# Causal convolution of a Mamba block moved from VectorE to ScalarE products and accumulating transfers

## The reference, cut to what matters

```python
x = x + 0.5 * ffn(layernorm(x))      # 8 experts, all dense: silu(x Wg) * (x Wu) Wd, weighted per row
x = x + mamba(layernorm(x))
x = x + 0.5 * ffn(layernorm(x))      # the same weights again
```

```python
xs, z = jnp.split(x @ W_in, 2, axis=-1)
xc = silu(depthwise_conv(xs, conv_w, 4 taps, causal) + conv_b)   # the change is here
dbl = xc @ W_x                                                   # 64 for dt, 16 for B, 16 for C
dt = softplus(dbl[:, :64] @ W_dt + b_dt)
h_t = exp(dt * A) * h_(t-1) + (dt * xc) * B_t                    # 16 states a channel
y = (sum over states of h_t * C_t + xc * D) * silu(z)
out = y @ W_out
```

## Time and profile before

| | before |
|---|---|
| three runs, us | 1270.12, 1273.47, 1273.81 (median 1273.47) |
| span of the profiled execution, us | 1272.6 |
| PE busy, us (share of the span) | 1253.2 (98%) |
| DVE busy | 1114.1 (88%) |
| ACT busy | 926.6 (73%) |
| POOL busy | 394.3 (31%) |
| chain that ended last, by engine | PE 73%, DVE 8%, DMA 8%, issue 5%, ACT 3%, POOL 2% |
| DMA: bytes moved, mean rate | 182.96 MB, 144 GB/s |
| queue of GpSimd's transfers, share of the 16 engines | 45.9% |
| mean granted TensorE clock | 0.998 |

### The profile page before, as it was taken

The page is one execution under the profiler, slowest core; times in us unless marked ns, Lnnn a source line. Parts: engine busy times, 40 slices in busy tenths (PEclk is TensorE's granted clock), DMA queues, the critical chain, the costliest instruction groups (busy, mean ns, idle before and its releaser), DMA issues.

```text
span 1272.6 us, 21027 instructions
## 1 busy us (share of the span) xinstructions
PE 1253.2 (98%) x7584; PEld 1096.0 (86%) x7584; DVE 1114.1 (88%) x1481; ACT 926.6 (73%) x1778; POOL 394.3 (31%) x459
## 2 busy tenths in 40 slices
PE   7999999999999999999999999999999999999998
PEld 5888888888888888888888888888888888888887
DVE  4544899989999999999999999999999989999433
ACT  5645978978886978877968788798867968654421
POOL 0101333334342423343333433333334333332110
PEclk9999999999999999999999999999999999999999
DMA  8211677777788868787987878887978887895111
GB/s 244 52 26 30 146 155 154 147 154 158 152 180 164 170 132 183 159 165 161 180 177 150 166 164 176 158 168 148 186 157 167 163 165 142 163 183 107 35 33 33
DMA packets 109303, 182.96 MB, mean 144 GB/s; under 512 B 11024, under 2 KB 23824, under 8 KB 109200
## 3 DMA queue, kind: packets, MB, share of 16 engines
q0 software_dynamic: 56336, 102.79, 45.9%
q1 hardware_dynamic: 52864, 78.85, 24.7%
HBM read 76.22 MB, written 2.62 MB: 62 GB/s over the span
## 4 chain that ended last, share of the span: by engine, by line
PE 73%; DVE 8%; DMA 8%; issue 5%; ACT 3%; POOL 2%; SPq 0%; DVEq 0%; POOLq 0%; ACTq 0%
PE PS L700 27%; PE PS L643 14%; PE PS L646 14%; PE PS L644 14%; DMA Y<-HS 5%; DVE HB L825 2%; DVE HS L923 2%; DMA XS<-DX 2%; DVE HS L931 1%; PE PS L730 1%; PE PS L715 1%; DVE HS L912 1%; PE PS L658 1%; POOL Y L1137 1%; DVE YE L818 1%
## 5 line engine op out<-in xcount | busy, mean ns | idle before, releaser
L700 PEld LDWEIGHTS PS<-WD,HB 128*128 128x128 f32 x4096 | 536.6, 191 | 44.0 <-issue 1.5
L700 PE MATMUL PS<-WD,HB 128*128 128x128 f32 x4096 | 540.1, 275 | 0.0
L1016 ACT ACTIVATE HB<-PS 128x512 f32<-128x512 f32 x512 | 294.3, 596 | 272.9 <-PE PS L646 270.8
L825 DVE TENSOR_TENSOR HB<-PS,HB 128x512 f32<-128x512 f32 x512 | 348.7, 682 | 119.2 <-PE PS L646 110.9
L1137 POOL DMA_DIRECT2D Y<-HS x252 | 221.1, 972 | 383.7 <-DVE HS L931 262.7
L1120 POOL DMA_DIRECT2D XT<-YE x126 | 117.9, 936 | 433.2 <-DVE YE L818 407.4
L643 PE MATMUL PS<-XH,WG 128*128 128x512 f32 x512 | 244.5, 478 | 3.3 <-ACT XH L996 2.3
L643 PE MATMUL PS<-XH,WU 128*128 128x512 f32 x512 | 204.9, 400 | 0.0
L646 PE MATMUL PS<-XH,WG 128*128 128x512 f32 x512 | 203.2, 397 | 0.6 <-DVE XH L883 0.6
L646 PE MATMUL PS<-XH,WU 128*128 128x512 f32 x512 | 202.1, 395 | 0.0
L644 PE MATMUL PS<-XH,WG 128*128 128x512 f32 x512 | 201.0, 393 | 0.0
(11 more groups left out here) (109 smaller groups left out, 1080.9 us busy)
## 6 DMA issues: line engine op xcount, KB each, us to landing
BCB<-BCD SPq DMA_DIRECT2D x128, 512.0 KB, 5.3
Y<-HS POOLq DMA_DIRECT2D x252, 256.0 KB, 6.4
XT<-YE POOLq DMA_DIRECT2D x126, 256.0 KB, 4.4
XS<-DX POOLq DMA_DIRECT2D x7, 512.0 KB, 9.2
XT<-in_L_attn_x_dram SPq DMA_DIRECT2D x8, 256.0 KB, 6.5
WD<-in_L_ffn_w_down_dram SPq DMA_DIRECT2D x8, 256.0 KB, 4.8
out_dram<-XT SPq DMA_DIRECT2D x8, 256.0 KB, 5.6
HS<-in_L_ffn_w_gate_dram SPq DMA_DIRECT2D x6, 256.0 KB, 4.0
```

The lines of the kernel that those rows point to most:

```text
L700: z = pe.matmul(expert(g)[:, j, :], HB[:, i % NH, j * P:(j + 1) * P], WD[:, e, c, :], start=c == 0 and j == 0, stop=c == FC - 1 and j == S ...
L825: v.tensor_tensor(H, up(i), H, ALU.mult).then_inc(S["v_h"], 1)
L1016: a.activation(HB[:, i % NH, :], gate(i), ACT.Silu).then_inc(S["a_sil"], 1)
```

## The change

For tiles 1 to 7 the multiply-adds of `b_conv` on DVE are replaced. Tile 0 keeps them. For each tap q = 0, 1, 2 and half j, ACT writes a product XS[q : q + 512] * tap q into a new buffer TP[q, j] (`b_tap`). GpSimd adds them with accumulating transfers of 128 x 512 f32, which is 256 KB: TP[0, j] += TP[1, j], and Y[j] += TP[2, j], both issued in `b_tap`; then, once both have landed, Y[j] += TP[0, j] (`b_sum`). The semaphore `c_cv0` or `c_cv1` counts the three landings of its half; `b_silu` waits for all three, and `b_sum` for the first two. `b_dt` waits for ACT's own products (`a_cv`) before XS is overwritten. In the planner a product costs .72 on ACT and needs a `calm()`, a transfer .95 on GpSimd and 5.0 more until it has landed. There are now a `yield` after each product and each sum, and an `until(at)` for the landing before the sums.

```diff
@@ before(t)
         for q in range(3):
             for j in range(2):
+                if t:
+                    yield from calm()
+                    at = step("b_tap", t, q, j, after=win_at, a=.72)
+                    if q:
+                        clock["p"] = max(clock["p"], at) + .95
+                        at = clock["p"] + 5.0
+                    yield True
+                    continue
                 at = step("b_conv", t, q, j, v=.67)
                 if q != 1:
                     yield True
             if q < 2:
                 bk = yield from take()
                 give(bk[0], "a_win", 4 * t + q + 3, step("b_in", t, q + 2, bk, pe=.69, a=.52))
+                yield True
+        if t:
+            yield from until(at)
+            for j in range(2):
+                at = step("b_sum", t, j, p=.95) + 5.0
                 yield True
         yield from until(at - .5)
@@ macaron_program
+        TP = sb("TP", [P, 3, 2, T])
@@ ACT
+                elif k == "b_tap":
+                    _, t, q, j = s
+                    wt.wait_ge(S["a_win"], 4 * t + 2)
+                    wt.wait_ge(S["v_halo"], 2 * t + 1)
+                    if t > 1:
+                        wt.wait_ge(S[f"c_cv{j}"], 16 * 3 * (t - 1))
+                    a.activation(TP[:, q, j, :], XS[:, t % 2, j, q:q + T], ACT.Copy, scale=cw_t[:, j, q:q + 1]).then_inc(S["a_cv"], 1)
                 elif k == "b_silu":
                     _, t, j = s
                     y = Y[:, t % 2, j, :]
-                    wt.wait_ge(S["v_cv"], 6 * t + 4 + j + 1)
+                    if t:
+                        wt.wait_ge(S[f"c_cv{j}"], 16 * 3 * t)
+                    else:
+                        wt.wait_ge(S["v_cv"], 4 + j + 1)
                     a.activation(y, y, ACT.Silu, bias=cb_t[:, j:j + 1]).then_inc(S["a_yc"], 1)
@@ ACT, b_dt
-                    wt.wait_ge(S["v_cv"], 6 * t + 6)
+                    if t:
+                        wt.wait_ge(S["a_cv"], 6 * t)
+                    else:
+                        wt.wait_ge(S["v_cv"], 6)
@@ GpSimd
+                elif k == "b_tap":
+                    _, t, q, j = s
+                    if q:
+                        wt.wait_ge(S["a_tap"], 2 * t + j + 1)
+                        wt.wait_ge(S["a_cv"], 6 * (t - 1) + 2 * q + j + 1)
+                        to = TP[:, 0, j, :] if q == 1 else Y[:, t % 2, j, :]
+                        gp.dma_start(to, TP[:, q, j, :], accum_op=ALU.add).then_inc(S[f"c_cv{j}"], 16)
+                elif k == "b_sum":
+                    _, t, j = s
+                    wt.wait_ge(S[f"c_cv{j}"], 16 * (3 * t - 1))
+                    gp.dma_start(Y[:, t % 2, j, :], TP[:, 0, j, :], accum_op=ALU.add).then_inc(S[f"c_cv{j}"], 16)
```

More of the change, by code:

```diff
@@ L499, in macaron_program @@
         S = {}
-        for n in ("c_small c_con c_wr c_acc c_y0 c_y1 c_bcd c_dt o_x init w_hi w_lo dv "
+        for n in ("c_small c_con c_wr c_acc c_y0 c_y1 c_bcd c_dt c_cv0 c_cv1 a_cv o_x init w_hi w_lo dv "
                   "m_g m_u m_dn m_tr m_lg m_win m_wx m_wt m_wo "
```

## The result

The changed kernel takes 1320.31 us (median of four runs, 1319.5 to 1323.3) against 1273.17 us for the kernel before (1270.12 to 1273.81). The ratio is 1.038, 95% interval 1.037 to 1.040: 47 us slower. The direction was forecast, the size was not: 1287 us and a range up to 1305. The span of the profiled execution is 1317.9 us, 45.3 more than before.

What follows compares the result with a forecast made beforehand. PE's full queue was taken as the bound, with DVE's chain just below. From 1272.6 us: minus 1 for DVE's relief, plus 9 for W_x stalls, plus 6 for the last tile, 1286.6, stated as 1287; range 1273 to 1305.

Steps and rivals of the forecast that it cites:

- The bound: Over the whole kernel, PE's queue sets the end; other engines' gains can return at most 9.5 us.
- ACT's products at nothing: 42 products on ACT, 30.3 us in all, fit its free time through calm() and cost 0.
- The chain after the last product: In each convolution, from last product towards W_x: two landings and one issue, 13.7 us, bounds 7.5 and 22.7.
- The stalls at W_x: PE waits at W_x for landings longer than planned: 1.3 us in each of 7 tiles, 9 us, bounds 0 and 28.
- Tiles 2 to 6 "no harm": In tiles 2 to 6 a later convolution does no harm, since their scans were not waiting for DX.
- Rival 3: Transfers served late, GpSimd and ACT queues held up, PE losing 3 us or more per tile: about 1308 us; chance 0.16.
- The last tile: Tile 7 has no slack: its scans start 8 us later, costing 6 us at the end, bounds 0 to 12.
- the 6 us between W_x and DX: In tile 7, W_x to DX shrinks by 6 us from 29.3, as tile 6's scans end sooner; between 0 and 8.
- DVE's relief at 1 us: DVE loses 31.3 us of multiply-adds; with PE full, only 1 us of PE's 9.5 us of waits is credited.
- my own two terms, 28 and 12 us: Upper bounds of the PE stalls at W_x over seven tiles (28) and the last tile's wait at the end (12).

Runs made afterwards that it cites:

- e13: The changed kernel with the calm() before each product taken out and nothing else: 1305.2 us, ratio 1.028 to the kernel before.
- e12: The changed kernel's work relisted: products one after another, three calm() instead of six, W_in's z chunks during the landings, usual turns: 1295.8 us, ratio 1.019.
- e6: The list of the kernel before with the changed work: products on ACT, accumulating transfers, nothing planned for landings: 1354.8 us, ratio 1.065.
- e5: The changed kernel's list, but DVE keeps the multiply-adds, with no products and no added transfers: 1330.5 us, ratio 1.046.
- e2: The change for tiles 1 to 6 only; tile 7 keeps DVE's multiply-adds: 1323.7 us, ratio 1.041 to the kernel before.
- e1: The change for tile 7 alone; tiles 0 to 6 keep DVE's multiply-adds: 1295.9 us, ratio 1.019 to the kernel before.
- e7: The changed kernel's work relisted: products one after another, three calm(), z chunks during the landings, every turn until W_x: 1292.7 us, ratio 1.017.
- e3: The kernel before plus 42 accumulating 256 KB transfers on GpSimd's queue into a buffer nothing reads: 1278.5 us, ratio 1.005.

## Why the prediction was right or wrong

**The bound.** Right. PE was full, a gain on DVE could not pay, and everything that makes PE wait would be paid in full. The sign followed from that.

**ACT's products at nothing.** This is the step that failed most. I wrote that calm() "puts a product only where ACT is at most 0.9 us ahead of PE" and that it costs nothing while ACT has 22 to 31 us free in 130. ACT's load was as forecast (952.7 us). But a wait for a gap costs the stream its time, not ACT: the products lie 30.9 us apart from first to last, 16.6 without calm() (e13), and the multiply-adds lay 15.5 apart. The gap from 1023.85 to 1040.32 in the rows above is one such wait, by the clocks of `timetable()` 13.7 us for the second product alone. Without calm() (e13) 15 of 47 us come back; with three of them, half the turns given away and no bank between (e12) 24.

**The chain after the last product.** I took 13.7 us from 6.4 us landings. The landings were near that, though with a longer tail, here for `b_tap` and then for `b_sum`:

```profile
DMA to landing us min/median/max: 4.1/6.6/13.2
...
DMA to landing us min/median/max: 4.7/7.2/8.2
```

The hardware's part of the chain was smaller, 9.2 us (e6), and the chain as it ran was longer, 18.7: `until(at)` and the turns given away make 15.5 of it even with nothing to land (e5). I sized the transfer from rows and forgot the list that waits for it. The fit in the Trainium skill ("DMA: Bandwidth & Descriptors", section "Anatomy of one DMA"), which gives an estimate of 2.6 us, is far from these medians of 6.6 and 7.2 in this kernel's traffic; the measurement decides.

**The stalls at W_x.** Forecast 9 us, 1 to 3 us "in most tiles". Measured: 5.2 us for the SiLU and 2.5 for another reader of the bank, in tiles 3, 4 and 7, against none before. The term is of the right size. Not foreseen, and put at nothing in the sum: the clock after the waits. PE was idle 3.17 us before W_x of tile 4. In the six microseconds from 661 the granted clock was 0.54, which is nearly the lower level of 1.2 GHz, and then 1.00 again (timeline, then stretches as above):

```profile
660.86 3.70 PE L729 MATMUL PS<-Y,WX 128*96 128x512 f32 x4 [3.17 <-ACT Y L1067]
...
661.00:667.00 6.00, 6.00 (x13) 3.27 (x14) 1.91 (x2) 2.42 (x5) 1.72 (x2) 0.54 0.61 105
...
667.00:680.00 13.00, 13.00 (x83) 11.52 (x82) 12.85 (x15) 9.16 (x16) 3.47 (x4) 1.00 0.84 170
```

The four W_x matmuls took 3.70 us there in place of 1.88, and the sixteen of W_out after the wait of 24 us 3.71 in place of 1.95; the granted clock was 0.69 from 1219.4 to 1225. The mean clock fell from 0.998 to 0.984, and PE was busy 7.7 us longer.

**Tiles 2 to 6 "no harm".** Wrong, and it is the second failed step. I compared DX of tile 5 with the closing product of tile 4 and found 22 us of slack. What DX has to beat is the last readout of tile 4, at 785.97, so the slack was 12 us, against 33.5 us more of chain. And I left out tile 1, which had none. Even 22 us would hold for one tile delayed alone. But `before(t + 1)` may start only after the scans of tile t have begun, so a delay larger than the slack is passed on: 21 us at the closing product of tile 1 have become 50 at that of tile 6. e2 shows what it costs: tile 7 untouched, 1323.7 us. Rival 3 named a build-up on the queues, from landings of 8.5 us on. The medians stayed at 6.3 to 7.2; the build-up was in the streams.

**The last tile.** Forecast: DX 8 us later and 6 us at the end. Measured: 52 us later by the clock of the run, and a wait of 24.1 us. e1, with tile 7 alone, has DX 29 us later (1080.0) and a wait of 19.7. The mechanism was the right one, the term mis-sized by the two steps above. The planner's waits behind the first product make 28 us. The copy of the halo just before the first product was 20.5 us late, which the tiles before had passed on; in e1 it was on time, and the first product 16 us late, with its calm() in between. That the 6 us between W_x and DX would come back was wrong for the changed kernel, 29.6 us against 29.3 before; in e7 it is 22.3, so there all of it came back.

**DVE's relief at 1 us.** Right while PE is the bound. In the kernel as changed the scans are the bound. There e5, the same list without the relief and without the added work, is 10 us slower: the relief is worth at least that much more than the work costs.

**The range.** It ended at 1305. The bounds that I gave for my own two terms, 28 and 12 us, reach 1311.6, and they too stop short of 1320: the lateness that every tile hands on was in no term.

## What to carry to other kernels

When a list or a planner decides the order, cost a new step by what the planner makes of it too: every conditional wait, every turn given away and every contested buffer that stands between the pieces, times their number. ACT's free time says that the work fits, not when it is done. And slack seen in one tile covers one delayed tile. Where each tile may start only after the one before, add the new latency to the whole chain from one tile's scans to the next one's, and compare that with the time that the scans take: here 109 us became 132, against 121.

## What was not expected of the hardware

- Two accumulating transfers in a row, the second issued on the first's landing, took 7.7 to 10.5 us from the end of the last product to the SiLU (e6), less than two medians of 6.4 us, while PE and what is queued behind stood still; the second took 3.6 us in the median. In the changed kernel, in company, they took 4.1 to 13.2 us each.
- 42 accumulating transfers of 256 KB that nothing waits for cost 5.3 us (e3). The trace shows them delaying another queue's store and loads.
- 3.17 us of idle PE were followed by some microseconds at 0.54 of the clock; after 1.58 us of idle PE at W_out of tile 4 (833.76) the sixteen matmuls took 2.02 us against 1.95, that is no slowdown of this size.
